# Second attention of a small decoder: two heads of each group of four are scaled by VectorE in place of GpSimd

## The chip, the cores and the metric

The kernel runs on one core of a Trainium2 chip, in one launch. The metric is the device time of that core in microseconds (us). A core has engines that work side by side, each through its own list of instructions in order, and semaphores join them: TensorE (PE in the profile, PEld its weight loads), VectorE (DVE), ScalarE (ACT), GpSimd (POOL) and SyncE (SP), which issues the DMAs.

## The reference

A decoder with two layers works on x of 8 batches x 100 tokens x 256 and a context of 8 x 361 x 256. In order: a state-space layer, a first cross attention, a mixture of 8 experts, four Mamba layers, a second cross attention, and a fake-quantised feed-forward layer, each with a residual and a layer norm behind it. The change is in the second cross attention, with 16 heads of width 16:

```
def _L1_xattn_ref(q, k, v, mask, Wq, bq, Wk, bk, Wv, bv, Wo, bo):
    ...
    scores = jnp.einsum('bhqd,bhkd->bhqk', qh, kh) / math.sqrt(D_K)
    scores = jnp.where(mask == 0, -jnp.inf, scores)
    attn = jax.nn.softmax(scores, axis=-1)
    attn = jnp.nan_to_num(attn, nan=0.0)
    x = jnp.einsum('bhqk,bhkd->bhqd', attn, vh)
    x = x.transpose(0, 2, 1, 3).reshape(bs, sq, HIDDEN)
    return x @ Wo + bo
```

## The kernel before, in words

The stages follow each other: the first attention with the experts until some 370 us into the span, the Mamba layers until some 1055, the second attention until some 1285, the feed-forward layer until the end.

Both attentions are software pipelines over heads. Four heads are a **quad**; a batch has four quads, and the 8 batches have quads 0 to 31. A quad's scores are four PSUM tiles of 100 x 361, one for each head. One step `g` of the loops `pe_attn`, `act_attn`, `dve_attn` and `pool_attn` is one head (`n, i = divmod(g, 4)`: quad n, head i), and each engine's instructions are issued in the order of these steps. In the second attention (`a.layer == 1`) the work of quad n runs as follows.

- **TensorE**, step i = 0: scores of quad n (L634, eight 32x361 products and then the mask, four bf16 products); it first waits until all four exponentials of quad n-1 are done (`a.exp_ready`), as they read the same PSUM tiles. Then the values of quad n-2 (24 products of 128x32 by 128x100). Steps 1 to 3: the transposes of quad n-1's probabilities, four a step (L705, called r0, r1, r2 here). r0 reads heads 0 and 1; r1 heads 1 and 2; r2 heads 2 and 3. They wait for the scaled heads on `a.prob_ready`, one semaphore for heads 0 and 1 and one for heads 2 and 3.
- **VectorE**, step 0: the negative maximum over heads 0 and 1 of quad n (L1088), then the scale factors for heads 2 and 3 of quad n-1 (reciprocal of the sum, L1079, and its product with a flag that is zero for a fully masked row, L1082), then the maximum over heads 2 and 3 of quad n (L1088 again). Step 2: the factors for heads 0 and 1 of quad n.
- **ScalarE**: the exponential of each head (L869, with its sum; it waits for the maximum of its pair), and between them the copies of the transposed probabilities out of PSUM (L879), in the order exp 0, exp 1, copy 0, exp 2, copy 1, exp 3, copy 2.
- **GpSimd**: multiplies each head's 100 x 361 exponentials by its factor in place (`pool_scale`, L972), heads 2 and 3 of quad n-1 in step 0 of quad n and heads 0 and 1 of quad n in step 2, each time behind `a.rs_ready`.

Beside this each batch has work at fixed steps, in every engine's own order: keys (steps 0 and 1), the mask (2), the query rows with their norm (2 to 9: L1163, the root on GpSimd L608 to L614, the end of the norm L621, a residual on GpSimd L977), values (steps 10, 13, 14; L1054 takes them out of PSUM), the output product and its norm (L1151 in step 6, L621 in step 8), the queries' copy to SBUF (L1061, step 9), the turn of a tile by TensorE (L747, steps 7 and 11), and, in steps 3 and 11 from batch 1 on until nine pieces are done, the quantising of a feed-forward weight (L2176 to L2185), all on VectorE where nothing else is said. Keys, values, queries, transposes and turned tiles share three PSUM banks in rotation; each waits until the third one before it has been read.

In the first attention VectorE scales all heads itself: reciprocal (L1073), and two `tensor_scalar` (L1076), with the same place in the order of steps. `step(ins)` lets VectorE wait until that instruction of its own has completed.

Of the kernel before, what the change touches and what calls it, by code (L numbers as in the profile page):

```python
# [5 lines left out]
ALU = mybir.AluOpType  # L6
# [8 lines left out]
B, S, D = 8, 100, 256  # L15
SK = 361
# [32 lines left out]
QUAD = 4  # L49
# [179 lines left out]
def decoder(nc, inp, out):  # L229
    ctx = ExitStack()  # L230
    with ctx:
# [3 lines left out]
        def sb(name, shape, dt=F32):  # L235
            return ctx.enter_context(nc.sbuf_tensor(name, shape, dt))
# [127 lines left out]
        anyv = sb("anyv", [P, 4])  # L364
# [11 lines left out]
        def pre(g, at):  # L376

            k, r = divmod(g - at, H)
            return (k + 1,) if r == 0 and 0 <= k + 1 < B else ()

        def fin(g, at):

            k, r = divmod(g - at, H)
            return (k - 1,) if r == 0 and 0 <= k - 1 < B else ()
# [23 lines left out]
        def has_quad(n):  # L408
            return 0 <= n < B * QUADS
# [159 lines left out]
        def step(ins):  # L569

            vstep.mark(ins)
            vstep.settle()
# [23 lines left out]
        def norm_root(pool, par, many=1, table=stat):  # L596

            G_ = nc.gpsimd
            st = table[0:S, par:par + many]
            var, v, y, t = (st[:, :, k:k + 1] for k in (7, 8, 9, 10))  # L600
            n = norms.rooted = norms.rooted + 1

            def mark(ins, k):
                ins.then_inc(n_step, 1)
                pool.wait_ge(n_step, 5 * (n - 1) + k)

            pool.wait_ge(n_stat, n)
            mark(G_.tensor_scalar(v, var, LN_EPS, 1.0, ALU.add, ALU.mult), 1)  # L608
            mark(G_.tensor_tensor(y, v, cst[0:S, 3:4].rearrange("p (o a) -> p o a", o=1).to_broadcast([S, many, 1]),
                                  ALU.pow), 2)  # L610
            mark(G_.tensor_tensor(t, y, y, ALU.mult), 3)
            mark(G_.tensor_tensor(t, t, v, ALU.mult), 4)
            mark(G_.tensor_scalar(t, t, -0.5, 1.5, ALU.mult, ALU.add), 5)
            G_.tensor_tensor(y, y, t, ALU.mult).then_inc(n_root, 1)  # L614
# [349 lines left out]

        def pool_scale(pool, a, n, i, k):

            pool.wait_ge(a.rs_ready, 2 * n + i // 2 + 1)
            for j in range(i, i + k):
                e = a.es[0:S, (n * QUAD + j) % 8, 0:SK]
                rs = hstat[0:S, n % 2, 2, j:j + 1]  # L970
                ready = a.prob_ready[j // 2]
                nc.gpsimd.tensor_scalar(e, e, rs, 1.0, ALU.mult, ALU.mult).then_inc(ready, 1)  # L972

        def gp_residual(pool, a, b):

            pool.wait_ge(a.in_ready, b + 1)
            nc.gpsimd.tensor_tensor(x_tok[:, b, :], a.x1[0:S, b % 2], bob[:, :], ALU.add).then_inc(xo2, 1)  # L977

        def pool_attn(pool, a):

            for g in a.steps:
                n, i = divmod(g, QUAD)
                if a.layer == 1 and i == 0 and has_quad(n - 1):
                    pool_scale(pool, a, n - 1, 2, 2)
                if a.layer == 1 and i == 2 and has_quad(n):
                    pool_scale(pool, a, n, 0, 2)
                if a.layer == 0:
                    for b in pre(g, AT["xo"]):
                        pool.wait_ge(xt_full, b + 1)
                        nc.gpsimd.tensor_tensor(x_tok[:, b, :], x_tok[:, b, :], bob[:, :], ALU.add).then_inc(xo_ready, 1)  # L990
                    for at in ("N1", "N2"):
                        for b in fin(g, AT[at]):
                            norm_root(pool, b % 2)
                    if g == AHEAD["gN"]:
                        gm_root_first(pool)
                        gm_rates(pool, 0)
                    if g == AHEAD["gD"]:
                        for c in range(CD):
                            gm_delta(pool, 0, 0, c)
                    if g == AHEAD["gB"]:  # L1000
                        pool.wait_ge(a.so_free, 4 * B)
                        gm_bx(pool, 0)
                else:
                    for b in pre(g, AT["1x"]):
                        norm_root(pool, b % 2)
                    for b in pre(g, AT["1xe"]):
                        gp_residual(pool, a, b)
                    for b in fin(g, AT["1N"]):
                        norm_root(pool, b % 2)
# [21 lines left out]
        def pool_front(pool):  # L1031
            pool_bias_parts(pool)
            for b in range(B):
                norm_root(pool, b % 2)
            pool.wait_ge(ld_attn, 16 * N_ATTN)
            pool_attn(pool, attn[0])
            mam_pool(pool)
            attn1_pool(pool)
            ffn_pool(pool)
# [27 lines left out]
        def dve_scale(dve, a, n, i, k):  # L1067

            dve.wait_ge(a.exp_ready, n * QUAD + i + k)
            st = hstat[0:S, n % 2]  # L1070
            if a.layer == 0:

                step(nc.vector.reciprocal(st[:, 2, i:i + k], st[:, 1, i:i + k]))  # L1073
                for j in range(i, i + k):
                    e = a.es[0:S, (n * QUAD + j) % 8, 0:SK]
                    nc.vector.tensor_scalar(e, e, st[:, 2, j:j + 1], CLIP_EPS, ALU.mult,  # L1076
                                            ALU.max).then_inc(a.prob_ready[j // 2], 1)
            else:
                step(nc.vector.reciprocal(st[:, 3, i:i + k], st[:, 1, i:i + k]))  # L1079

                bp = n // QUADS % 2
                nc.vector.tensor_scalar(st[:, 2, i:i + k], st[:, 3, i:i + k], anyv[0:S, bp:bp + 1], None,  # L1082
                                        ALU.mult).then_inc(a.rs_ready, 1)

        def dve_max(dve, a, n, i):

# [728 lines left out]
        def gm_root_first(pool):  # L1815

            s = msq[0:S]
            t, r0, tmp = s[:, 12:16], s[:, 8:12], s[:, 16:20]
            power = cst[0:S, 3:4].to_broadcast([S, GB])
            pool.wait_ge(m_rs, 1)  # L1820
            nc.gpsimd.tensor_scalar(t, s[:, 0:4], 1.0 / D, LN_EPS, ALU.mult, ALU.add).then_inc(m_root, 1)
            pool.wait_ge(m_root, 1)
            nc.gpsimd.tensor_tensor(r0, t, power, ALU.pow).then_inc(m_root, 1)
            pool.wait_ge(m_root, 2)
            nc.gpsimd.tensor_tensor(tmp, r0, r0, ALU.mult).then_inc(m_root, 1)
            pool.wait_ge(m_root, 3)
            nc.gpsimd.tensor_tensor(tmp, t, tmp, ALU.mult).then_inc(m_root, 1)
            pool.wait_ge(m_root, 4)
            nc.gpsimd.tensor_scalar(tmp, tmp, -0.5, 1.5, ALU.mult, ALU.add).then_inc(m_root, 1)
            pool.wait_ge(m_root, 5)  # L1830
            nc.gpsimd.tensor_tensor(nrm4[0:S, :], r0, tmp, ALU.mult).then_inc(m_rstd, 5)

        def gm_rates(pool, l):

            pool.wait_ge(m_alog, l + 1)
            nc.gpsimd.tensor_scalar(aneg[:, l % 2], aneg[:, l % 2], -1.0, -SLOWEST, ALU.mult, ALU.min).then_inc(m_aneg, 1)

        def gm_delta(pool, m, g, c):

            if m == 0:  # L1840
                pool.wait_ge(m_soft, 1)
            else:
                p_read(pool, m, f"D{c}")
                pool.wait_ge(m_bx, UNITS * (m - 1) + NQ * (c + 1))
            nc.gpsimd.tensor_tensor(dx[:, c], delta[g][:, c], xc[g][:, c], ALU.mult).then_inc(m_dx, 1)
            pool.wait_ge(m_dx, CD * m + c + 1)
            nc.gpsimd.memset(delta[g][:, c].rearrange("p (b t) -> p b t", b=GB)[:, :, 0:1], RESET).then_inc(m_first, 1)

        def gm_bx(pool, unit):

            m, u = divmod(unit, UNITS)
            c, nq = divmod(u, NQ)
            if c == 0:
                pool.wait_ge(m_bin[nq], 16 * (m + 1))
            wait(pool, m_scan, 2 * (unit - BX + 1))
            nc.gpsimd.tensor_tensor(  # L1856
                bx[:, unit % BX].rearrange("p (j t) -> p j t", j=SEGMENT),
                bbc[:, nq].rearrange("p (j t) -> p j t", j=SEGMENT),
                dx[:, c].rearrange("p (o t) -> p o t", o=1).to_broadcast([P, SEGMENT, GT]),
                ALU.mult).then_inc(m_bx, 1)  # L1860
# [616 lines left out]
```

## Time and profile before

| | us |
|---|---|
| median of 3 runs | 1352.81 |
| lowest, highest | 1341.77, 1353.56 |
| the profiled execution's own time | 1346.96 |
| its span, first to last instruction | 1345.1 |
| mean granted TensorE clock in it | 0.942 |
| busy: TensorE / VectorE / ScalarE / GpSimd | 1155.2 / 1092.8 / 826.3 / 820.9 |

The span is cut by the stages above; the busy times are sums over stages whose limits differ. A releaser in square brackets behind a row is what ended the idle time before it.

### The profile page before, as it was taken

The page shows a single profiled execution, that of the slowest core. Times are in us where ns is not written, and L with a number is a line of the kernel's source. Part 1 is how long each engine was busy: PE and PEld are TensorE (multiplying, and loading weights), DVE is VectorE, ACT ScalarE, POOL GpSimd, SP SyncE. Part 2 cuts the span into 40 slices and gives each one's busy share as a digit, 9 for nine tenths or more (in the row PEclk, how much of TensorE's full clock was granted, in tenths as well). Part 3 has the DMA queues.
Part 4 walks back from the last instruction along what each step waited for, and adds up shares of the span by engine and source line. Part 5 has one row for each costly group of instructions (what it writes and reads, how often), then busy time and mean ns, then how long its engine had stood idle before and what let it go on. Part 6 is the DMA issues. An engine that isn't in the chain of part 4 may idle for free.

```text
span 1345.1 us, 17666 instructions
## 1 busy us (share of the span) xinstructions
PE 1155.2 (86%) x6026; PEld 671.9 (50%) x6026; DVE 1092.8 (81%) x1618; ACT 826.3 (61%) x1825; POOL 820.9 (61%) x743
## 2 busy tenths in 40 slices
PE   7798888878579998989989989899987888888874
PEld 3455555544144554545545445455454555555544
DVE  3577777575599999999999999999999667676556
ACT  1555555564366777767777678776764355566664
POOL 6001111100498998999989989899899344445405
PEclk9899999989779999999999999999998989899885
DMA  6000002000500504106032060230500300000000
GB/s 202 12 12 12 12 12 70 1 1 3 219 15 15 225 1 169 45 0 239 1 121 92 1 240 1 80 133 1 197 31 0 80 16 17 22 27 2 1 1 25
DMA packets 22142, 79.15 MB, mean 59 GB/s; under 512 B 4935, under 2 KB 8847, under 8 KB 21138
## 3 DMA queue, kind: packets, MB, share of 16 engines
q1 hardware_dynamic: 22054, 78.02, 16.8%
q8 instruction: 49, 0.80, 0.2%
q14 instruction: 39, 0.32, 0.1%
HBM read 76.77 MB, written 1.24 MB: 58 GB/s over the span
## 4 chain that ended last, share of the span: by engine, by line
PE 38%; DVE 33%; ACT 13%; POOL 8%; issue 7%; DMA 1%; SPq 0%; ACTq 0%; DVEq 0%; POOLq 0%
PE ps L634 35%; DVE ps L1941 10%; DVE arena L1946 6%; POOL arena L1856 4%; DVE arena L1944 4%; DVE hstat L1088 3%; ACT ps L1740 3%; ACT L629 2%; ACT arena L869 2%; PE ps L705 2%; POOL arena L1868 2%; DVE arena L1906 2%; ACT arena L879 1%; DMA arena<-in_exb 1%; ACT arena L1626 1%
## 5 line engine op out<-in xcount | busy, mean ns | idle before, releaser
L634 PE MATMUL ps<-arena 128*32 128x100 f32 (+8 forms) x3300 | 522.3, 385 | 84.0 <-ACT arena L869 25.5
L1856 POOL TENSOR_TENSOR arena<-arena 128x1600 f32<-128x1600 f32 x128 | 456.5, 3581 | 34.9 <-DVE ps L1941 21.8
L634 PEld LDWEIGHTS ps<-arena 128*32 128x32 f32 (+7 forms) x3300 | 262.7, 147 | 301.8 <-issue 112.5
L634 PE MATMUL ps<-arena,ident 128*128 128x400 f32 x1024 | 378.4, 519 | 33.4 <-DVE arena L1944 17.5
L1740 ACT ACTIVATE ps<-arena 128x400 f32<-128x400 f32 x512 | 283.1, 590 | 194.4 <-DVE arena L1944 161.1
L1941 DVE TENSOR_TENSOR_SCAN ps<-ps,arena 128x800 f32<-128x800 f32 x176 | 320.7, 1822 | 18.6 <-ACT ps L1740 14.4
L634 PEld LDWEIGHTS ps<-arena,ident 128*128 128x128 f32 x1024 | 197.5, 196 | 197.3 <-POOL arena L1868 24.0
L869 ACT ACTIVATE arena<-ps,hstat 100x361 f32<-100x361 f32 x256 | 143.5, 563 | 108.5 <-DVE hstat L1088 108.3
L608 POOL TENSOR_SCALAR stat<-stat 100x1 f32<-100x1 f32 (+1 forms) x44 | 8.6, 196 | 293.3 <-DVE stat L589 292.1
L1944 DVE TENSOR_TENSOR arena<-ps,arena 128x800 f32<-128x800 f32 x176 | 174.4, 991 | 6.0
L1088 DVE TENSOR_REDUCE hstat<-ps 100x2 f32<-100x722 f32 x128 | 115.6, 905 | 75.0 <-PE ps L634 74.6
L1868 POOL TENSOR_TENSOR arena<-arena 128x1600 f32<-128x1600 f32 x40 | 143.1, 3577 | 15.1 <-DVE arena L1946 15.0
L972 POOL TENSOR_SCALAR arena<-arena,hstat 100x361 f32<-100x361 f32 x128 | 71.7, 573 | 113.3 <-DVE hstat L1082 112.3
L1946 DVE TENSOR_TENSOR_SCAN arena<-ps,arena 128x800 f32<-128x800 f32 x80 | 140.3, 1804 | 0.2 <-issue 0.2
L705 PE MATMUL ps<-ident,arena 100*128 100x100 f32 x768 | 105.6, 264 | 16.3 <-POOL arena L972 8.0
L879 ACT ACTIVATE arena<-ps 128x400 f32<-128x400 f32 x192 | 97.1, 506 | 33.8 <-PE ps L705 32.3
L705 PEld LDWEIGHTS ps<-ident,arena 100*128 100x128 f32 x768 | 82.5, 147 | 48.2 <-issue 18.4
L629 ACT ACT_TABLE_LOAD x63 | 80.8, 1283 | 1.1
L634 PE MATMUL ps<-wv,arena 128*128 128x256 f32 (+1 forms) x192 | 53.2, 402 | 5.9 <-DVE arena L1054 3.4
L869 ACT ACTIVATION_READ_ACCUMULATOR arena<-ps,hstat 100x1 f32 x256 | 52.3, 204 | 0.0
L634 PE MATMUL ps<-arena,wk 128*128 128x361 f32 x128 | 48.7, 508 | 0.7
L1076 DVE TENSOR_SCALAR arena<-arena,hstat 100x361 f32<-100x361 f32 x128 | 46.5, 406 | 2.3
(191 smaller groups left out, 1004.1 us busy)
## 6 DMA issues: line engine op xcount, KB each, us to landing
arena<-bc_scratch SPq DMA_DIRECT2D x64, 800.0 KB, 6.5
arena<-in_ctxT SPq DMA_DIRECT2D x16, 361.0 KB, 3.8
arena<-in_w_in SPq DMA_DIRECT2D x4, 1024.0 KB, 4.9
arena<-in_expT SPq DMA_DIRECT2D x1, 2048.0 KB, 12.7
arena<-in_w_out SPq DMA_DIRECT2D x4, 512.0 KB, 3.2
arena<-in_mask SPq DMA_DIRECT2D x8, 141.0 KB
arena<-in_xT SPq DMA_DIRECT2D x2, 400.0 KB, 4.1
x_tok<-in_x_tok SPq DMA_DIRECT2D x1, 800.0 KB
```

Of the source, the lines that this page charges most:

```text
L629: act.add_instruction(mybir.InstLoadActFuncSet(name=nc.get_next_instruction_name(), act_func_set_id=which, engine=mybir.EngineType.Activat ...
L634: return nc.tensor.matmul(outp, lhsT, rhs, start=first, stop=last)
L705: last = nc.tensor.transpose(ps[:, a.bank(b, name), k * S:(k + 1) * S], a.es[0:S, (n * QUAD + i) % 8, kc * P:(kc + 1) * P], ident[0:S, 0:S])
L869: nc.scalar.activation(a.es[0:S, v % 8, 0:SK], ps[0:S, i, 0:SK], ACT.Exp, bias=hstat[0:S, n % 2, 0, i:i + 1], scale=1.0, accum_out=hstat[0 ...
L879: nc.scalar.activation(a.aT[:, n % 2, r * QUAD * S:(r + 1) * QUAD * S], ps[:, a.bank(b, name), 0:QUAD * S], ACT.Copy).then_inc(a.freed(b, ...
L1088: nc.vector.tensor_reduce(hstat[0:S, n % 2, 0, i:i + 2], ps[0:S, i:i + 2, 0:SK], AX.X, ALU.max, negate=True).then_inc(a.max_ready, 1)
L1740: last = nc.scalar.activation(psf[:, half_at(k) + j * GT:half_at(k) + (j + 1) * GT], delta[g][:, c], ACT.Exp, scale=aneg[:, l % 2, n:n + 1])
L1856: nc.gpsimd.tensor_tensor(bx[:, unit % BX].rearrange("p (j t) -> p j t", j=SEGMENT), bbc[:, nq].rearrange("p (j t) -> p j t", j=SEGMENT), ...
L1868: nc.gpsimd.tensor_tensor(h, h, cbc[:, nq], ALU.mult).then_inc(m_cmp, 1)
L1941: nc.vector.tensor_tensor_scan(a, a, bx[:, unit % BX, w], 0.0, ALU.mult, ALU.add).then_inc(m_scan, 1)
L1944: nc.vector.tensor_tensor(y, a, cbc[:, nq, w], ALU.mult).then_inc(m_cmd, 1)
L1946: nc.vector.tensor_tensor_scan(y, a, bx[:, unit % BX, w], 0.0, ALU.mult, ALU.add).then_inc(m_scan, 1)
```

## The change

VectorE gives the factors of heads 0 and 1 to GpSimd as before. For heads 2 and 3 of each quad it waits for its own factor and does the two multiplications itself (step 0 of the next quad), with the completion semaphore on each of them; GpSimd leaves them out. `rs_ready` is counted once a quad. Line numbers behind L1080 move by five, those inside `dve_scale` otherwise: the reciprocal is L1077 and the factor L1080 in the changed kernel, the new multiplications L1088, the maxima L1093.

```
         def pool_scale(pool, a, n, i, k):
-            pool.wait_ge(a.rs_ready, 2 * n + i // 2 + 1)
+            pool.wait_ge(a.rs_ready, n + 1)
             for j in range(i, i + k):
                 e = a.es[0:S, (n * QUAD + j) % 8, 0:SK]
                 rs = hstat[0:S, n % 2, 2, j:j + 1]
...
                 n, i = divmod(g, QUAD)
-                if a.layer == 1 and i == 0 and has_quad(n - 1):
-                    pool_scale(pool, a, n - 1, 2, 2)
                 if a.layer == 1 and i == 2 and has_quad(n):
                     pool_scale(pool, a, n, 0, 2)
...
-                nc.vector.tensor_scalar(st[:, 2, i:i + k], st[:, 3, i:i + k], anyv[0:S, bp:bp + 1], None,
-                                        ALU.mult).then_inc(a.rs_ready, 1)
+                scale = nc.vector.tensor_scalar(st[:, 2, i:i + k], st[:, 3, i:i + k], anyv[0:S, bp:bp + 1], None,
+                                                ALU.mult)
+                if i == 0:
+                    scale.then_inc(a.rs_ready, 1)
+                    return
+                step(scale)
+                for j in range(i, i + k):
+                    e = a.es[0:S, (n * QUAD + j) % 8, 0:SK]
+                    nc.vector.tensor_scalar(e, e, st[:, 2, j:j + 1], None, ALU.mult).then_inc(a.prob_ready[j // 2], 1)
```

On VectorE, around step 0 of the second quad of a batch (L621 there ends the norm of the query rows; `hstat` holds the maxima and factors, `arena` the exponentials). Before:

```order
L2185 TENSOR_SCALAR arena<-arena 88x1024
L1088 TENSOR_REDUCE hstat<-ps 100x2
L1079 RECIPROCAL hstat<-hstat 100x2
L1082 TENSOR_SCALAR hstat<-hstat,anyv 100x2
L1088 TENSOR_REDUCE hstat<-ps 100x2
L621 TENSOR_SCALAR arena<-arena,stat 100x256
L1079 RECIPROCAL hstat<-hstat 100x2
L1082 TENSOR_SCALAR hstat<-hstat,anyv 100x2
L1151 TENSOR_TENSOR arena<-ps,x_tok 100x256
```

And in the changed kernel:

```order
L2190 TENSOR_SCALAR arena<-arena 88x1024
L1093 TENSOR_REDUCE hstat<-ps 100x2
L1077 RECIPROCAL hstat<-hstat 100x2
L1080 TENSOR_SCALAR hstat<-hstat,anyv 100x2
L1088 TENSOR_SCALAR arena<-arena,hstat 100x361 x2
L1093 TENSOR_REDUCE hstat<-ps 100x2
L621 TENSOR_SCALAR arena<-arena,stat 100x256
L1077 RECIPROCAL hstat<-hstat 100x2
L1080 TENSOR_SCALAR hstat<-hstat,anyv 100x2
L1156 TENSOR_TENSOR arena<-ps,x_tok 100x256
```

The two multiplications stand between the two maxima of every quad but the first (and behind the last quad's factors at the end); nothing else on VectorE moves.

On GpSimd, the same place, from the end of the root of the query rows' norm. Before:

```order
L614 TENSOR_TENSOR stat<-stat 100x1
L972 TENSOR_SCALAR arena<-arena,hstat 100x361 x2
L977 TENSOR_TENSOR x_tok<-arena,bob 100x256
L972 TENSOR_SCALAR arena<-arena,hstat 100x361 x2
L608 TENSOR_SCALAR stat<-stat 100x1
```

And in the changed kernel:

```order
L614 TENSOR_TENSOR stat<-stat 100x1
L977 TENSOR_TENSOR x_tok<-arena,bob 100x256
L972 TENSOR_SCALAR arena<-arena,hstat 100x361 x2
L608 TENSOR_SCALAR stat<-stat 100x1
```

The first pair of L972 has gone there; the pair for heads 0 and 1 stays where it was.

## Rows read from the trace of the kernel before

**Rows 1.** The page: the chain that ended last, share of the span by engine.
```profile
PE 38%; DVE 33%; ACT 13%; POOL 8%; issue 7%; DMA 1%; SPq 0%; ACTq 0%; DVEq 0%; POOLq 0%
```

**Rows 2.** Windows, the second attention: length, busy (instructions) by engine, clock, DMA.
```profile
1060.00:1283.00 223.00, 189.90 (x1797) 126.14 (x1796) 148.93 (x381) 128.44 (x391) 100.79 (x219) 0.93 0.09 25
```

**Rows 3.** Waits, 1060 to 1290: waiter <- releaser: total us, times, longest.
```profile
PE ps L634 <- ACT arena L869: 11.4, 9, 1.4
PE ps L705 <- POOL arena L972: 8.0, 10, 1.1
PE ps L747 <- DVE arena L1151: 4.6, 6, 0.8
```

**Rows 4.** Timeline, quad 30: start, us, engine, line, operation [idle before <-releaser].
```profile
1268.61 0.91 DVE L1088 TENSOR_REDUCE hstat<-ps 100x2 f32<-100x722 f32 x1 [1.98 <-PE ps L634]
1269.43 0.15 DVE L1079 RECIPROCAL hstat<-hstat 100x2 f32<-100x2 f32 x1
1269.55 0.56 ACT L869 ACTIVATE arena<-ps,hstat 100x361 f32<-100x361 f32 x1 [2.25 <-DVE hstat L1088]
1269.62 0.23 DVE L1082 TENSOR_SCALAR hstat<-hstat,anyv 100x2 f32<-100x2 f32 x1
1269.76 0.90 DVE L1088 TENSOR_REDUCE hstat<-ps 100x2 f32<-100x722 f32 x1
1269.96 1.12 POOL L972 TENSOR_SCALAR arena<-arena,hstat 100x361 f32<-100x361 f32 x2 [1.32 <-DVE hstat L1082]
...
1270.58 1.02 PE L705 MATMUL ps<-ident,arena 100*128 100x100 f32 x6 [0.69 <-POOL arena L972]
...
1271.03 0.57 ACT L869 ACTIVATE arena<-ps,hstat 100x361 f32<-100x361 f32 x1
...
1271.94 0.59 ACT L869 ACTIVATE arena<-ps,hstat 100x361 f32<-100x361 f32 x1
...
1272.67 0.87 PE L634 MATMUL ps<-arena 32*100 32x361 f32 x8 [0.90 <-ACT arena L869]
```

**Rows 5.** Timeline, first attention, one step 0 and one L621.
```profile
72.89 0.73 DVE L1076 TENSOR_SCALAR arena<-arena,hstat 100x361 f32<-100x361 f32 x2
...
73.54 0.90 DVE L1088 TENSOR_REDUCE hstat<-ps 100x2 f32<-100x722 f32 x1
...
80.96 0.40 DVE L621 TENSOR_SCALAR arena<-arena,stat 100x256 f32<-100x256 f32 x1
```

**Rows 6.** Timeline, quad 13, second of its batch.
```profile
1157.82 0.64 DVE L621 TENSOR_SCALAR arena<-arena,stat 100x256 f32<-100x256 f32 x1
...
1159.76 0.57 PE L747 MATMUL ps<-ident,arena 100*128 100x100 f32 x2 [0.77 <-DVE arena L1151]
```

**Rows 7.** Timeline, quads 14 and 22, third of their batches.
```profile
1166.08 0.43 DVE L1061 SCALAR_TENSOR_TENSOR arena<-ps,bq,head_rows 128x200 f32<-128x200 f32 x1 [0.26 <-PE ps L634]
...
1166.68 0.43 DVE L1061 SCALAR_TENSOR_TENSOR arena<-ps,bq,head_rows 128x200 f32<-128x200 f32 x1 [0.17 <-PE ps L634]
...
1220.12 0.74 DVE L1061 SCALAR_TENSOR_TENSOR arena<-ps,bq,head_rows 128x200 f32<-128x200 f32 x2
...
1220.58 1.13 PE L634 MATMUL ps<-wv,arena 128*128 128x256 f32 x4
```

**Rows 8.** Timeline, end of quad 23, fourth of its batch, and quad 24.
```profile
1227.14 0.59 ACT L869 ACTIVATE arena<-ps,hstat 100x361 f32<-100x361 f32 x1
...
1227.96 0.87 PE L634 MATMUL ps<-arena 32*100 32x361 f32 x8
```

**Rows 9.** Timeline, quad 12, first of its batch, and the scores of quad 13.
```profile
1150.47 0.17 DVE L1079 RECIPROCAL hstat<-hstat 100x2 f32<-100x2 f32 x1 [1.15 <-ACT arena L869]
...
1151.38 0.55 ACT L869 ACTIVATE arena<-ps,hstat 100x361 f32<-100x361 f32 x1
...
1153.01 0.87 PE L634 MATMUL ps<-arena 32*100 32x361 f32 x8 [1.44 <-ACT arena L869]
```

**Rows 10.** One line's instructions (min/median/max ns): L1076 in the first attention.
```profile
L1076 DVE TENSOR_SCALAR arena<-arena,hstat x128: 396/406/441, 43.3 to 330.9; 100x361 f32<-100x361 f32 x128
```

## The prediction

> **What bounds the kernel now.** I read the page's chain first: the work that ended last is shared by TensorE with 38% and VectorE with 33% [rows 1]. Such shares mix stages, so I cut out the stage of the change with the windows view. In its 223 us TensorE is busy 189.9 us (85%), VectorE 148.9, GpSimd 100.8 [rows 2]. TensorE has 33 us without a matmul, and the view of waits tells for whom: 11.4 us for the exponentials L869, 8.0 us for GpSimd's scaling L972, 4.6 us for L1151 on VectorE before a turn [rows 3]. The 8.0 us are what the change is aimed at. Whether they are worth anything is read from the timeline of a quad.
>
> Quad 30 is a clean one [rows 4]. I count from the start of its first maximum at 1268.61. Factors for heads 2 and 3 of the quad before start at +1.01, the second maximum at +1.15, the third exponential at +2.42, the fourth at +3.33; it ends at +3.92, and the scores of the next quad start at +4.06, 0.14 behind it. TensorE waited 0.69 for GpSimd in this quad, and still stood 0.90 before the next scores, waiting for an exponential. So here the chain maximum, four exponentials, scores sets the pace, and the wait for GpSimd lies inside it. The change puts work between the two maxima of that chain.
>
> **The price of the two multiplications on VectorE.** The factor L1082 starts at +1.01 and takes 0.23, and a dependent VectorE instruction starts 0.04 behind the end of the one that it waits for (1269.43 + 0.15 to 1269.62) [rows 4]: the multiplications start at +1.28. The first attention has the same multiplication on the same shape, with one more operation: 406 ns each [rows 10], and from the start of two of them to the next maximum 0.65 (72.89 to 73.54) [rows 5]. The second maximum then starts at +1.93 where it started at +1.15: **0.78 us later** in every quad. From a maximum's start to its exponential is 0.94 (1268.61 to 1269.55) [rows 4]; the third exponential can start at +2.87 in place of +2.42: **0.45 later**, as the remaining 0.33 was slack on ScalarE. What is bought: head 2 is ready at about +1.28 + 0.41 = +1.69, where GpSimd's first half of 1.12 us from +1.35 ended at +1.91; r1 can start 0.2 earlier.
>
> A rule that would make it cheaper is in the Trainium skill, GPSIMD Engine Reference, Key points: VectorE is about twice as fast for elementwise work. By it two heads would take half of GpSimd's 1.12, 0.56 in place of the 0.65 that the row shows, and each quad's delay would shrink by 0.09, the sum by some 2 us. The first attention's rows, 406 against some 560 ns a head, speak against two to one, and I go by them.
>
> **A gain on the side.** L621, a multiplication with two scalars, takes 0.64 while GpSimd's L972 runs beside it, as in quad 13 [rows 6], and 0.40 in the first attention, where GpSimd stands idle at that moment [rows 5]. L621 follows the second maximum in the second and third quad of each batch. With the pair for heads 2 and 3 gone from GpSimd it should take 0.40: 0.24 back. GpSimd's own queue gets shorter by 64 instructions of some 560 ns; but it waits for VectorE nearly everywhere, so that is worth nothing by itself. DMAs and SyncE are not touched.
>
> **Quad by quad.** The pattern repeats with the batch; I went through all 32 quads in the timeline.
>
> - *First quad of a batch* (4, 8, ..., 24: six). Keys keep TensorE and ScalarE busy: the third exponential starts at 1151.38, 4.11 behind the first maximum, and VectorE stands idle 1.15 before its next factor [rows 9]. Both covers are wider than 0.78. Cost 0. Were the cover gone, it would be 0.45 each.
> - *Second quad* (5, 9, ..., 25: six). VectorE goes without a gap from the second maximum through L621, the factors and L1151, and the turn on TensorE waits 0.77 for it at 1159.76 [rows 6]; six times in the stage [rows 3]. The next scores come straight behind. So the 0.78 lands whole, less the 0.24 of L621: 0.54. The exponentials' way gives less. 6 x 0.54 = 3.24.
> - *Third quad* (10, 18, 22, 26). L621 is followed by L1061, whose first half ends at about 1220.53, and the product for the values, which needs that bank, starts at 1220.58 [rows 7]. Again 0.54: 4 x 0.54 = 2.16. In quads 6 and 14 TensorE was at half clock and VectorE waited twice for it there, 0.26 and 0.17 in quad 14 [rows 7], so about 0.54 - 0.26 - 0.17, or 0.12, is left: 0.24. Quad 2 has no L621, and L1061 had more room: 0.23. Together 2.63.
> - *Fourth quad* (3, 7, ..., 27: seven). The last exponential ends at 1227.73, the scores start at 1227.96 [rows 8], 0.23 behind in place of the least 0.14: slack 0.09. 0.45 - 0.09 = 0.36; 7 x 0.36 = 2.52.
> - *The last batch* (28, 30, 31) has the clean chain of quad 30: 3 x 0.45 = 1.35. In 29 ScalarE is late by itself: 0. In quads 0 and 1 the stage is still filling: 0.
>
> Sum: 3.24 + 2.63 + 2.52 + 1.35 = **9.7 us slower**. The profiled execution took 1346.96, 1.9 more than its span, which the change leaves alone: 1356.7. The median shown, 1352.81, lies 5.9 above the profiled one, for a reason that this page doesn't show; from it the sum gives 1362.5. I take the middle, **1360**. Against either base it is +0.7%. A difference of about 1% (13.5 us) is what a measurement of this kernel tells from none.
>
> The granted clock is 0.93 here [rows 2]; halved pieces of it fall on some quads. A slower chain may move them, by a few us either way. I put no sum on it, only range.
>
> **The rivals.**
>
> *A. GpSimd's lateness set the pace: faster.* TensorE did wait 8.0 us in ten places for L972 [rows 3]. If those waits, and not the exponentials, decided, and VectorE had room, the change would take away up to those 8.0 us, and 14 times 0.24 of L621, 3.4: -11.4, 1335.6 on the profiled base, 1341 on the median. It decides if the second maximum is not what the third exponential waits for, so if ScalarE is the later one by over 0.78. Against it: in quad 30 the maximum ended at 1270.66 and the exponential started at 1271.03, only 0.37 behind, and the wait before the scores came after the one for GpSimd [rows 4]. Half of this effect beside some of the cost would give about no change. Chance 0.15.
>
> *B. Everything lands.* VectorE has stretches without a gap before the maxima (L2185 and then L1088 in the order shown). If the slacks are used up once the whole pattern shifts, each quad pays 0.78: 32 x 0.78 = +25, 1372 on the profiled base, 1378 on the median. Against it: the idle 1.15 and the late exponentials in the first quads [rows 9], which recur in each batch whatever the rest does. Chance 0.15.
>
> *C. The multiplications are slower here than in the first attention*, where GpSimd rests. As L621 stretched from 0.40 to 0.64, each could take 0.24 more, the delay 1.26 in place of 0.78, and the sum some 9.7 x 1.26 / 0.78 = 15.7 and a little more: 1363 to 1369. It needs a GpSimd instruction beside them; but at +1.28 to +2.0 only the pair that is removed ran there [rows 4], and roots and residuals lie elsewhere. Chance 0.06.
>
> The Trainium skill, GPSIMD Engine Reference, Key points, has the contention with VectorE in its two-port mode, which is what the 0.64 of L621 would be; it says nothing of how much.
>
> *D. The change does nothing visible*, since TensorE, busy 85%, catches up in the first quad of each batch, whose TensorE stands idle 1.44 before the scores [rows 9]. But that idle time waits for an exponential that itself waits for TensorE's work, so it moves with the start of the quad. Sum 0: 1347 to 1353. Chance 0.07.
>
> My forecast, +6 to +13, has the remaining 0.57.
>
> **Range and chances.** Runs of the kernel before lie between 1341.77 and 1353.56, so the forecast's own range is 1351 to 1367. With D and the upper half of A taken in below and most of B above: 1347 to 1374. Slower by over 1%: B 0.15, most of C 0.05, and 0.08 of the forecast by spread, together 0.28. Faster by over 1%: only A in full, 0.04. Within 1%: 0.68.
>
> **What the profile after should show.** L1088 (the new one) 64 times at about 406 ns, starting 0.27 behind the start of L1080. From the first maximum of a quad to the second 1.93 in place of 1.15. Third exponential at +2.87 in the clean quads; in the first quads of batches still near +4.1. L621 at 0.40 instead of 0.64 in the stage. The waits of L705 for L972 nearly gone, those of L634 for L869 longer, the turn L747 behind L1156 waiting 0.5 longer. The stage about 10 us longer, nothing changed before 1060 and behind it. Wrong would be: exponentials that start as before (A), gaps of VectorE gone in the first quads (B), multiplications near 640 ns (C), or a stage as long as before (D).

## The result, and the profile after

The changed kernel took 1358.79 us in the median of 13 runs beside 1346.93 for the kernel before: ratio 1.0096, 95% interval 1.0074 to 1.0117. That is some 13 us slower, between 10 and 16. A second comparison gave 1.0096 again (1.0072 to 1.0121). The ratios are of fast runs; one run of the kernel before took 1524.38 us and is left out of them. The prediction said +9.7 us on either base, 1360 with 1347 to 1374, and 0.68 for "within 1%". The direction was right and the sum too small. Two things came out better than the sum by luck. The 1360 stood on a base of some 1350, the middle between 1346.96 and the 1352.81 of the first three runs, which is 3 us above the 1346.93 of thirteen; that made up for the 3 us missing from the sum. And 0.96% lies just inside "within 1%", with an interval that reaches beyond it.

The profiled span went from 1345.1 to 1357.3 us. Quad 30 after, in the timeline, answers to [rows 4] (L1156 of the changed kernel is the L1151 of before, L1059 the L1061, L1052 the L1054):

```profile
1277.66 0.91 DVE L1093 TENSOR_REDUCE hstat<-ps 100x2 f32<-100x722 f32 x1 [1.99 <-PE ps L634]
...
1278.67 0.23 DVE L1080 TENSOR_SCALAR hstat<-hstat,anyv 100x2 f32<-100x2 f32 x1
1278.94 0.72 DVE L1088 TENSOR_SCALAR arena<-arena,hstat 100x361 f32<-100x361 f32 x2
...
1279.40 0.79 PE L705 MATMUL ps<-ident,arena 100*128 100x100 f32 x6 [0.47 <-DVE arena L1088]
1279.58 0.90 DVE L1093 TENSOR_REDUCE hstat<-ps 100x2 f32<-100x722 f32 x1
...
1280.40 0.40 DVE L621 TENSOR_SCALAR arena<-arena,stat 100x256 f32<-100x256 f32 x1
1280.52 0.56 ACT L869 ACTIVATE arena<-ps,hstat 100x361 f32<-100x361 f32 x1 [0.32 <-DVE hstat L1093]
...
1282.16 0.56 PE L634 MATMUL ps<-arena 32*100 32x361 f32 x4 [0.91 <-ACT arena L869]
```

Counted from the first maximum at 1277.66, the multiplications start at +1.28, the second maximum at +1.92, and the third exponential at +2.86; ScalarE is now idle before it, waiting for that maximum. The next scores start at +4.50 where they started at +4.06. The transposes of head 2, the second part of r1, start at +1.74 in place of +1.97, and that buys nothing: TensorE stands as long before the scores as it did (0.91). L621 takes 0.40 where it took 0.64. The waits of the stage answer to [rows 3]:

```profile
PE ps L634 <- ACT arena L869: 16.2, 16, 2.0
PE ps L747 <- DVE arena L1156: 7.8, 6, 1.3
PE ps L705 <- DVE arena L1088: 5.5, 9, 0.8
```

TensorE's wait for the scaled heads fell from 8.0 us (for GpSimd) to 5.5 (for VectorE); its waits for exponentials rose by 4.8 and the turn's by 3.2. The three places of the prediction, in the timeline of the changed kernel, a second and a third quad [rows 6, 7]:

```profile
1249.90 0.36 PE L747 MATMUL ps<-ident,arena 100*128 100x100 f32 x2 [1.29 <-DVE arena L1156]
...
1254.90 0.75 DVE L1059 SCALAR_TENSOR_TENSOR arena<-ps,bq,head_rows 128x200 f32<-128x200 f32 x2
...
1255.37 1.13 PE L634 MATMUL ps<-wv,arena 128*128 128x256 f32 x4 [0.38 <-DVE arena L1059]
```

The turn waits 1.29 where it waited 0.77, and the value product now waits for L1059. The end of a fourth quad and a first quad [rows 8, 9]:

```profile
1235.61 0.56 ACT L869 ACTIVATE arena<-ps,hstat 100x361 f32<-100x361 f32 x1
...
1236.41 0.87 PE L634 MATMUL ps<-arena 32*100 32x361 f32 x8 [0.55 <-ACT arena L869]
...
1241.26 0.17 DVE L1077 RECIPROCAL hstat<-hstat 100x2 f32<-100x2 f32 x1 [0.38 <-ACT arena L869]
...
1243.81 0.56 PE L634 MATMUL ps<-arena 32*100 32x361 f32 x4 [1.44 <-ACT arena L869]
```

In the first quad VectorE is still idle for 0.38 us of the 1.15, and TensorE's wait is the 1.44 of before: the cover held.

**A table of periods.** A period is the time from the first maximum of a quad to that of the next, in us, from the timelines, in quads of which no part ran at half clock. The quad's number is in brackets. Batch 6 (quads 24 to 27) is free of the quantising that lengthens other quads; "clean" is quad 30, or quads 28 and 29 where 30 was partly at half clock.

| kernel | first (24) | second (25) | third (26) | fourth (27) | clean |
|---|---|---|---|---|---|
| before | 7.40 | 5.86 | 6.22 | 5.80 | 5.71 |
| the change | 7.40 | 6.39 | 6.76 | 6.24 | 6.15 |
| heads 2, 3 unscaled | 7.39 | 5.71 | 6.13 | 5.80 | 5.72 |
| both maxima first | 7.39 | - | - | 5.83 | 5.74 |
| L1151 moved (GpSimd scales) | 7.40 | 5.71 | 6.22 | 5.80 | 5.71 |
| all three ways | 7.40 | 5.74 | 6.44 | 5.83 | 5.74 |
| multiplied twice | 7.40 | - | - | 6.87 | - |

"-" marks quads that were partly at half clock there.

### The profile page after: what moved, and what is told of

Read it like the earlier page. It is cut to its first block, busy times and chain, and to the rows that moved or that the text cites. A ratio compares the mean times of both kernels' runs of the same rounds, so it can differ in the third digit from the quotient of the medians.

```text
span 1357.3 us, 17666 instructions
## 1 busy us (share of the span) xinstructions
PE 1157.3 (85%) x6026; PEld 673.2 (50%) x6026; DVE 1111.7 (82%) x1682; ACT 828.1 (61%) x1825; POOL 786.2 (58%) x679
## 4 chain that ended last, share of the span: by engine, by line
PE 38%; DVE 37%; ACT 13%; issue 7%; POOL 4%; DMA 1%; SPq 0%; ACTq 0%; DVEq 0%; POOLq 0%
PE ps L634 35%; DVE ps L1946 10%; DVE arena L1951 7%; DVE hstat L1093 5%; DVE arena L1949 4%; ACT ps L1745 3%; ACT L629 2%; POOL arena L1861 2%; ACT arena L869 2%; PE ps L705 2%; DVE arena L1911 2%; DVE arena L1088 1%; ACT arena L1631 1%; POOL arena L1873 1%; ACT arena L879 1%
## 5 line engine op out<-in xcount | busy, mean ns | idle before, releaser
L634 PE MATMUL ps<-arena 128*32 128x100 f32 (+8 forms) x3300 | 522.2, 384 | 87.7 <-ACT arena L869 30.7
L1861 POOL TENSOR_TENSOR arena<-arena 128x1600 f32<-128x1600 f32 x128 | 456.5, 3581 | 34.7 <-DVE ps L1946 21.5
L634 PEld LDWEIGHTS ps<-arena 128*32 128x32 f32 (+7 forms) x3300 | 263.2, 147 | 304.9 <-issue 110.8
L634 PE MATMUL ps<-arena,ident 128*128 128x400 f32 x1024 | 378.3, 519 | 33.6 <-DVE arena L1949 17.5
L634 PEld LDWEIGHTS ps<-arena,ident 128*128 128x128 f32 x1024 | 197.5, 196 | 197.4 <-POOL arena L1873 24.1
L869 ACT ACTIVATE arena<-ps,hstat 100x361 f32<-100x361 f32 x256 | 143.2, 562 | 116.6 <-DVE hstat L1093 116.5
L1093 DVE TENSOR_REDUCE hstat<-ps 100x2 f32<-100x722 f32 x128 | 115.6, 904 | 75.8 <-PE ps L634 75.4
L705 PE MATMUL ps<-ident,arena 100*128 100x100 f32 x768 | 104.1, 263 | 15.4 <-DVE arena L1088 5.5
L972 POOL TENSOR_SCALAR arena<-arena,hstat 100x361 f32<-100x361 f32 x64 | 36.3, 580 | 138.2 <-DVE hstat L1080 137.3
L705 PEld LDWEIGHTS ps<-ident,arena 100*128 100x128 f32 x768 | 81.7, 146 | 46.7 <-issue 18.2
L634 PE MATMUL ps<-wv,arena 128*128 128x256 f32 (+1 forms) x192 | 54.2, 408 | 9.0 <-DVE arena L1052 3.5
L869 ACT ACTIVATION_READ_ACCUMULATOR arena<-ps,hstat 100x1 f32 x256 | 51.5, 201 | 0.0
L634 PE MATMUL ps<-arena,wk 128*128 128x361 f32 x128 | 49.9, 518 | 0.7
```

Source lines behind the costliest of these rows:

```text
L634: return nc.tensor.matmul(outp, lhsT, rhs, start=first, stop=last)
L705: last = nc.tensor.transpose(ps[:, a.bank(b, name), k * S:(k + 1) * S], a.es[0:S, (n * QUAD + i) % 8, kc * P:(kc + 1) * P], ident[0:S, 0:S])
L869: nc.scalar.activation(a.es[0:S, v % 8, 0:SK], ps[0:S, i, 0:SK], ACT.Exp, bias=hstat[0:S, n % 2, 0, i:i + 1], scale=1.0, accum_out=hstat[0 ...
L1093: nc.vector.tensor_reduce(hstat[0:S, n % 2, 0, i:i + 2], ps[0:S, i:i + 2, 0:SK], AX.X, ALU.max, negate=True).then_inc(a.max_ready, 1)
L1861: nc.gpsimd.tensor_tensor(bx[:, unit % BX].rearrange("p (j t) -> p j t", j=SEGMENT), bbc[:, nq].rearrange("p (j t) -> p j t", j=SEGMENT), ...
```

## The experiments

All ratios are to the kernel before, run beside them, with 95% intervals. The code shows the part of each edit that matters; "..." marks lines left out.

**Both maxima first.** In `dve_quad`, second attention only:

```
+            if i == 0 and has_quad(n) and a.layer == 1:
+                dve_max(dve, a, n, 2)
             if i == 0 and has_quad(n - 1):
                 dve_scale(dve, a, n - 1, 2, 2)
...
```

> The changed kernel with one thing moved: in the second attention both maxima of a quad stand ahead of the factors and multiplications for heads 2 and 3 of the quad before. My account has two ways in which the multiplications cost: through the second maximum to the third exponential (fourth quads of a batch 0.36 each, last batch 0.45 each, some 3.9 us together), and through VectorE's own queue to L1156 and L1059, for which TensorE waits (second and third quads, some 5.8 us). The first way should be gone: third exponential back at +2.42 from the first maximum, fourth quads back to 5.8 us, the kernel some 4 us faster than the changed one and still some 6 us slower than before. r1 waits longer, as head 2 is ready only at about +2.5, which may give back up to 0.2 us a quad in the last batch. Rival, that added VectorE time costs by its amount wherever it stands: as slow as the changed kernel, +12. Rival, that only the exponentials' way counts: equal to before.

Measured: 1.0075 (1.0045 to 1.0105), +6 to +14 us. In its timeline a fourth quad:

```profile
1254.98 1.73 DVE L1093 TENSOR_REDUCE hstat<-ps 100x2 f32<-100x722 f32 x2 [1.63 <-PE ps L634]
...
1257.08 0.73 DVE L1088 TENSOR_SCALAR arena<-arena,hstat 100x361 f32<-100x361 f32 x2
1257.39 0.57 ACT L869 ACTIVATE arena<-ps,hstat 100x361 f32<-100x361 f32 x1
```

The third exponential is back at +2.41 though VectorE does the same work, and the fourth and clean quads are back at 5.83 and 5.74. So the first way, through the second maximum, is shown by the periods. By time alone it is not: the run lies between the expected +6 and the change's +13, and its interval reaches both. In its profile all six second quads ran partly at half clock.

**Heads 2 and 3 left unscaled**, the factor signals TensorE:

```
-                step(scale)
-                for j in range(i, i + k):
-                    ...
+                scale.then_inc(a.prob_ready[1], 2)
```

> Heads 2 and 3 of each quad are scaled by no engine (this part of the computation is left out); the factor itself signals TensorE. It tells what GpSimd's scaling of these heads cost in the kernel before, and so the most that any mover of it could win. My account: TensorE's 8.0 us of waits for GpSimd lie inside the exponentials' chain and are worth nothing; what comes back is L621 at 0.40 in place of 0.64, in six second quads and four third ones, so 2.4 us faster than before, third exponential at +2.42 as before. Rival A of the prediction (GpSimd's lateness set the pace): 8 to 11 us faster than before.

Measured: 0.9981 (0.9960 to 1.0002), -2.6 us where -2.4 was expected. The agreement is closer than the mechanism allows: L621 is back at 0.40, but the second quads have 5.71 in place of 5.86, 0.15 less and not 0.24, and the third quads are 0.09 to 0.16 shorter (6.13 in place of 6.22 in quad 26, 7.25 in place of 7.41 in quad 14, against the kernel before once more). By periods that is some 1.7 us. The rest is as before. In its waits L705 no longer waits for GpSimd, and L634's wait for exponentials is 12.4 us where it was 11.4 [rows 3]:

```profile
PE ps L634 <- ACT arena L869: 12.4, 9, 2.0
...
PE ps L705 <- ACT arena L879: 7.3, 12, 0.8
```

Rival A, 8 to 11 us faster, falls: the interval ends at 5.4 us faster. By the periods, the scaling of these heads had some 1.7 us to give, wherever it is moved, and not the 8.0 of the view of waits.

**The multiplications done twice**, first into scratch:

```
...
+                    vstep.mark(nc.vector.tensor_scalar(hh[0:S, IC - 4 + j, 0:SK], e, st[:, 2, j:j + 1], None, ALU.mult))
...
```

> The changed kernel with the two multiplications of VectorE done twice, first into a scratch tile. Second maximum at +2.66 in place of +1.92 (0.73 more). My account: second quads 6 x 0.73, third quads 6 x 0.73, fourth quads 7 x 0.73, last batch 3 x 0.73, together 16.1; in the first quads VectorE's idle time of 0.38 is used up and 0.35 is over, which counts in the five batches in which VectorE goes on without a gap to the next quad's maximum: 1.8. So 18 us slower than the changed kernel, the third exponential at +3.6 in clean quads and still near +4.1 in first quads. Rival B (everything lands): 32 x 0.73 = 23. Rival, that most of the change's cost has nothing to do with the multiplications' time (an offset of another origin): clearly less than 18.

Measured: 1.0289 (1.0249 to 1.0329), 26 us above the change. The second pair costs 0.63 a quad in the order of VectorE, not 0.73 (starts at 1282.36 and 1282.99), and the fourth quads went from 6.24 to 6.87, so one for one:

```profile
1282.36 0.73 DVE L1088 TENSOR_SCALAR arena<-arena,hstat 100x361 f32<-100x361 f32 x2
...
1282.99 0.72 DVE L1091 TENSOR_SCALAR arena<-arena,hstat 100x361 f32<-100x361 f32 x2
...
1283.63 0.90 DVE L1096 TENSOR_REDUCE hstat<-ps 100x2 f32<-100x722 f32 x1
...
1284.57 0.56 ACT L869 ACTIVATE arena<-ps,hstat 100x361 f32<-100x361 f32 x1 [0.96 <-DVE hstat L1096]
```

For five of the first quads my expectation was 0.35; those with quantising that ran at full clock became 0.15 to 0.17 longer (quad 4: 9.00 in place of 8.84), and quad 24 kept its 7.40. By full-clock periods that makes some 15 us. In the profile the stage is 25 us longer than in the change's first profile and 21.5 longer than in its second; what goes beyond 15 lies in quads at half clock, of which there were 52 us here, against 17 and 37.5. My expectation of 18 had no term for that. By time alone the 26 is nearer to rival B's 23 than to my 18; the periods of the first quads speak against B.

**One instruction moved in the kernel before**: L1151 ahead of the factors for heads 0 and 1.

```
             for g in steps:
+                if a.layer == 1:
+                    for b in fin(g, AT["1N"]):
+                        dve_resid_add(dve, a, b)
                 dve_quad(dve, a, g)
```

> The kernel before (GpSimd scales all heads), with one instruction moved: in step 6 of a batch the addition that takes the output product out of PSUM (L1151) stands ahead of the factors for heads 0 and 1, not behind them. In the kernel before the turn on TensorE waits for it 0.77 in six second quads. It could start at the end of L621, 1158.46 in place of 1159.20 in quad 13, so 0.74 earlier: 6 x 0.74 = 4.4 us faster than before, if nothing else holds the turn; the turn also needs L621's result, which is there by then. Rival: the six waits are covered by something else (exponentials, which leave 0.35 in the second quads), then 6 x 0.35 = 2.1 at most. Rival, no effect, since the factors and GpSimd's scaling of heads 0 and 1 come 0.4 later and hold r0: 0 or slower.

Measured: 0.9986 (0.9960 to 1.0012). The turn no longer waits, but the scores behind it now wait 0.61 for an exponential, and the second quads end at 5.71:

```profile
1235.15 0.41 DVE L1151 TENSOR_TENSOR arena<-ps,x_tok 100x256 f32<-100x256 f32 x1
...
1235.70 0.36 PE L747 MATMUL ps<-ident,arena 100*128 100x100 f32 x2
...
1236.68 0.87 PE L634 MATMUL ps<-arena 32*100 32x361 f32 x8 [0.61 <-ACT arena L869]
```

My account, 4.4 us, was wrong. The first rival of the expectation holds, with 0.15 a quad in place of 0.35: a wait of 0.77 was worth 0.15, since the next one stood close behind. No quad of the kernel before gets below 5.71, the clean chain.

**The change once more.**

> The changed kernel as it is, once more. Two questions. The size: my sum is 9.7 us; the first comparison gave a ratio of 1.0096, 12.9 us. And where the profiled execution's 12.2 us lay: 2.2 before the second attention begins, 7.3 within it and 2.7 behind its last maximum. My account: only the part within belongs to the change, and it would be 9.3 with the clock's halved pieces of before; the parts before and behind are spread between executions, behind it with the length of half clock (0.2 us for each us of it). So here the quads at full clock should have the same periods to 0.02 us (7.40, 6.39, 6.76, 6.24 from first to fourth), and the parts before and behind should differ from 2.2 and 2.7. Rival, that the change costs something outside its stage: again some +2 and +3.

Measured: 1.0096 (1.0072 to 1.0121); full-clock periods the same to 0.01. The attention began at 1064.75 (before 1060.21, the first profile of the change 1062.40, all others 1058.1 to 1063.2, among them four with VectorE's multiplications at 1058.7 to 1060.0): spread, as far as this shows. But the part behind the last quad's first maximum was 73.5 us again, where I had expected it to differ: for that part the rival is not refuted. In the two profiles of the kernel before it was 70.8 and 71.8. See the point on the clock in the next section.

**GpSimd busy beside VectorE's multiplications**, on scratch:

```
...
+                if a.layer == 1 and i == 0 and has_quad(n - 1):
+                    pool.wait_ge(a.rs_ready, 2 * (n - 1) + 2)
+                    ...
+                        nc.gpsimd.tensor_scalar(hh[0:S, IC - 2 + j, 0:SK], hh[0:S, IC - 3, 0:SK], cst[0:S, 3:4], 1.0,
+                                                ALU.mult, ALU.mult).then_inc(beside, 1)
...
```

> The changed kernel, and GpSimd again does two multiplications of 100 x 361 at the old moment (behind the factor for heads 2 and 3), on scratch that nobody reads. So GpSimd works beside VectorE's two multiplications, which the prediction's rival C priced at 0.24 more for each. My account: L1088's successor shows some 640 ns in place of 406 (as L621 beside GpSimd did), the second maximum at some +2.4 in place of +1.92, and the kernel slower than the changed one by 0.48 in second, third and fourth quads and the last batch: 22 x 0.48 = 11 us. GpSimd's pair is over before L621, which stays near 0.40. Rival, that only some of VectorE's instructions are stretched beside GpSimd and this one not: same as the changed kernel.

Measured: 1.0136 (1.0113 to 1.0158), 5 us above the change, where I had expected 11. In the timeline (L1096 is the L1088 of the changed kernel, L988 GpSimd's new pair):

```profile
1265.09 1.04 DVE L1096 TENSOR_SCALAR arena<-arena,hstat 100x361 f32<-100x361 f32 x2
1265.14 1.41 POOL L988 TENSOR_SCALAR arena<-arena,cst 100x361 f32<-100x361 f32 x2 [2.22 <-DVE hstat L1087]
...
1266.97 0.56 ACT L870 ACTIVATE arena<-ps,hstat 100x361 f32<-100x361 f32 x1 [0.63 <-DVE hstat L1101]
```

The two multiplications take 1.04 together in place of 0.73, and GpSimd's two 1.41 in place of 1.12: both are stretched. Not each of them, though: VectorE's first, which starts 0.06 ahead of GpSimd's, takes 0.41 as it does alone, and its second 0.72. That is why the stretch is 0.31 a quad and not the 0.48 that I took from L621; the fourth quads went from 6.24 to 6.55. L621 stayed at 0.40. The mechanism of rival C exists, and the change doesn't meet it, since GpSimd's pair is gone. The Trainium skill, GPSIMD Engine Reference, Key points, says that GpSimd shares its SBUF interfaces with VectorE and contends with VectorE's instructions in a two-port mode. The run agrees that such instructions contend; which mode VectorE was in, no view shows.

**VectorE scales only where its work falls in a first quad** (`n % QUADS == QUADS - 1`), GpSimd all the rest. GpSimd's side of it:

```
...
-                if a.layer == 1 and i == 0 and has_quad(n - 1):
+                if a.layer == 1 and i == 0 and has_quad(n - 1) and n % QUADS:
...
```

> The kernel before, with VectorE scaling heads 2 and 3 only where its work falls in the first quad of a batch (the heads of the fourth quad before it, and at the very end), all other heads on GpSimd. It tests the cover of the first quads, in which the prediction set the cost at 0. My account: within 1 us of before, first quads 7.40 at full clock as before, though their second maximum starts 0.78 later; third exponential still at +4.1. Rival, that the delay is handed on through VectorE's gapless stretch to the next maximum: first quads 0.4 to 0.8 longer, 3 to 5 us.

Measured: 0.9991 (0.9969 to 1.0013). First quads 8.84, 8.60, 8.59, 8.14, 7.72, 7.40, each within 0.01 of before. So the cost of 0 there is shown. In the timeline the idle 0.38 is what is left of the cover:

```profile
1226.58 0.73 DVE L1096 TENSOR_SCALAR arena<-arena,hstat 100x361 f32<-100x361 f32 x2
1227.22 0.90 DVE L1101 TENSOR_REDUCE hstat<-ps 100x2 f32<-100x722 f32 x1
...
1228.50 0.17 DVE L1086 RECIPROCAL hstat<-hstat 100x2 f32<-100x2 f32 x1 [0.38 <-ACT arena L876]
```

**All three ways**, with VectorE doing all that it does in the change: both maxima first, L1151's addition early, and in the third quads

```
...
                     for b in pre(g, AT["1Qc"]):
                         dve_q(dve, a, b, b % 2)
+                    for b in fin(g - 1, AT["1Ne"]):
+                        norm_end(dve, b % 2, a.zt[0:S, b % 2], a.x2[0:S, b % 2], a.x_ready)
...
```

> VectorE does all that it does in the changed kernel, in an order that keeps it off the three paths I named: both maxima ahead of the multiplications, L1151's addition ahead of the factors for heads 0 and 1, and in the third quads the queries' copy (L1061 before) ahead of L621. My account: second quads 5.74 at full clock (before 5.86, change 6.39), third 6.4 (before 6.22, change 6.76), fourth 5.83 (before 5.80, change 6.24): in all within 1 us of before, some 9 to 12 faster than the change. Rival, that VectorE's added 24 us of work cost by their amount wherever they stand: as slow as the change.

Measured: 1.0016 (0.9992 to 1.0039). In batch 6 the periods are as expected, 5.74, 6.44, 5.83. The same 64 multiplications on the same engine cost 2 us here (-1 to 5) and 13 in the change. This is the strongest of the runs: most of the cost is the place in the order, not the added work itself. The first two ways are closed by it. The third is only shortened: in quad 26 L1059 starts at +2.74 (1244.32), where the change has +3.06, and the period is 0.22 above that of before. And a third quad with quantising gains nothing from the order. Of these, quad 14 ran at full clock here:

```profile
1161.43 1.73 DVE L1093 TENSOR_REDUCE hstat<-ps 100x2 f32<-100x722 f32 x2 [1.22 <-PE ps L634]
...
1168.90 0.69 DVE L2203 TENSOR_SCALAR arena<-arena 88x1024 bf16<-88x1024 f32 x1
1169.51 1.71 DVE L1093 TENSOR_REDUCE hstat<-ps 100x2 f32<-100x722 f32 x2
```

It has 8.08, where the kernel before has 7.41 and the change, by quad 6 with the same work, 7.96. In all three kernels VectorE has no gap in such a quad from one maximum to the next. There the added work costs 0.55 in one order and 0.67 in the other.

No version is faster than the kernel before by what could be measured: this one is not, and L1151 alone moved (0.9986) and VectorE in first quads only (0.9991) have 1 inside their intervals.

**Maxima first in the last batch alone.**

> The changed kernel, with both maxima ahead of the multiplications in the last batch alone (quads 28 to 31). In both profiles of the change, the part from the last quad's first maximum to the last norm's end of the attention took 16.0 us in place of 14.1, with 10.2 us of half clock in place of 3.4, and the feed-forward layer 57.5 in place of 56.6; my sum had 0.45 there. With both maxima first everywhere that part took 12.7, with no half clock. My account: quads 28, 30 and 31 get their 0.45 back (1.3 us), the last part goes back to 12.7 to 14.1 and the feed-forward layer to 56.6: together 3 to 5 us faster than the change, ratio to before about 1.006 to 1.007. Rival, that the drain's 2.3 us of half clock come from all the 24 us that VectorE's work was made longer, or from chance: only 1.3 us faster than the change, the last part still at 16.

Measured: 1.0116 (1.0075 to 1.0157), not faster than the change. In its profile the last part was 14.85 in place of 16.0 and the feed-forward layer 56.9 in place of 57.5: shorter, but not the 12.7 to 14.1 and 56.6 that I expected, and the time of the kernel doesn't bear even that out. Inconclusive.

**The kernel before once more.**

> The kernel before, once more, as the measure of what two profiles of the same program differ by. Expected: ratio 1.000 within 0.003, full-clock periods 7.40, 5.86, 6.22, 5.80 to 0.02, the part behind the last first maximum near 70.7, and the start of the attention somewhere between 1058 and 1062.

Measured: 0.9984 (0.9960 to 1.0008). Its periods agree, but its attention took 209.7 us where the first profile has 214.1:

```profile
1061.80:1271.50 209.70, 178.28 (x1724) 117.66 (x1726) 145.43 (x373) 123.49 (x377) 97.55 (x213) 0.97 0.10 26
```

The mean clock was 0.97 and 0.94 in that stretch (half clock for 11.6 and 27.3 us). The same program differs by 4 us in this stage, and all but some hundredths of it lies in quads that ran partly at half clock in one of the two or in both. The attention began at 1061.84, and the part behind the last quad's first maximum took 71.8 us where I had expected 70.7.

## Why the prediction was right, and what was mis-sized

- *What the change is aimed at.* Right: most of the 8.0 us of waits for GpSimd lay inside the exponentials' chain. The unscaled run gives 1.7 us by periods and 2.6 (-0.3 to 5.4) by time for them and L621's part together.
- *The price a quad.* Second maximum at +1.93, measured +1.92; third exponential at +2.87, measured +2.86; multiplications of 406 ns, measured 406 (400 to 411). L621 at 0.40, measured 0.40.
- *First quads: 0.* Right, in the change and where VectorE scales only there.
- *Second quads: 0.54.* Measured 0.53 (5.86 to 6.39). With L621's 0.24 taken off whole this is right, though the unscaled run, in which L621 is shorter too, won only 0.15: there the exponentials' way came next.
- *Third quads: 0.54, with 0.12 for quads 6 and 14.* 0.54 measured in 26, and 0.31 in quad 2 (5.96 to 6.27), for which I had 0.23. The 0.12 was wrong: VectorE's waits in quads 6 and 14 came from TensorE's half clock in that one execution. At full clock quad 14 of the kernel before has 7.41 (kernel before once more) and quad 6 of the change, with the same work, 7.96: 0.55 each, 0.86 more in all. What holds in these two is also another thing than the value product: VectorE works without a gap, and its next maximum starts 1.2 us after the scores that it reads are there. A stretch at half clock is no place to read slack from.
- *Fourth quads: 0.36.* Measured 0.44. I took 0.23 minus the least 0.14 between last exponential and scores as slack. The scores of the change wait for that exponential, [0.55 <-ACT arena L869], and still start 0.24 behind its end (1235.61 + 0.56 to 1236.41). The distance is 0.23 in all seven fourth quads of the kernel before, the change, and "both maxima first" alike, and 0.14 in the last batch; why it is longer is not known. So it was no slack: 7 x 0.08 = 0.56 more.
- *Last batch: quads 28, 30, 31, and 0 for 29.* At half clock in the profile, quad 29 looked late by itself; at full clock it has 5.72 before (kernel before once more). By the clean 6.15 of quad 30 it costs 0.43: 0.43 more.
- *The sum.* With these, at full clock: 6 x 0.53 + 6 x 0.54 + 0.31 (quad 2) + 7 x 0.44 + 4 x 0.43 = 11.5 us, against 9.7 predicted and 10 to 16 measured. The profiles bear out the part up to the last quad, 11.1 of it: from the first maximum of quad 0 to that of quad 31 it was 214.1 and 209.7 us before, 221.4 and 225.2 in the change, 11.4 more in the mean.
- *The clock, given range and no sum.* The remaining 1 to 2 us fit it, but are not settled. The window from the last first maximum to the end of the attention, before and in the two profiles of the change, in that order:

```profile
1274.30:1288.40 14.10, 9.96 (x148) 7.86 (x148) 3.84 (x12) 8.10 (x20) 4.83 (x12) 0.88 0.00 1
```
```profile
1283.80:1299.80 16.00, 11.64 (x148) 9.34 (x148) 5.21 (x16) 8.00 (x20) 2.63 (x8) 0.68 0.01 2
```
```profile
1290.00:1305.90 15.90, 11.66 (x148) 9.36 (x142) 5.17 (x16) 7.95 (x19) 2.61 (x8) 0.68 0.01 2
```

  It is 1.8 to 1.9 us longer, with 0.43 of it accounted for and the clock at 0.68 in place of 0.88. But the kernel before once more had 0.62 there and took 14.8, and the run made to test it did not get faster. Whether the change draws half clock onto this part, or two profiles fell alike, stays open.
- *Rivals.* A fell to the unscaled run. B fell to the first quads' unchanged periods, though quad 14 shows that a quad without a gap in VectorE's order pays in either order. C's mechanism is real but not met. D fell to 1.0096, with an interval that begins at 1.0074.

## What to carry to other kernels

The same work on the same engine cost 13 us or 2, by its place: before moving work to an engine with idle time, look at what stands behind it in that engine's order, and put it behind whatever another engine is waiting for. Where the engine has no gap at all, as in quad 14, neither order tried was free. A view of waits gives a wait's length, not its worth; the worth is what is gained before the next wait sets in (0.77 was worth 0.15 here). Read slack only in stretches at full clock. Take a gap between two steps as slack only if it gets smaller when the step before it is late: the 0.23 here did not.

## What the runs showed of the hardware

VectorE and GpSimd stretch each other on SBUF to SBUF multiplications with two such instructions each: 0.73 to 1.04 us for VectorE's pair, 1.12 to 1.41 for GpSimd's, with VectorE's first, which started ahead, not stretched (0.41) and its second at 0.72; L621 went from 0.64 to 0.40 when GpSimd's pair left. VectorE's maximum over PSUM was not stretched beside GpSimd's pair: 0.90 (1269.76) as in the changed kernel without it (1279.58). TensorE ran at 1.2 GHz for between 10 and 52 us of this one stage in twelve profiles, and two profiles of the same program differed by 16 us of it and 4 us of time (the kernel before), and by 20 and 4 (the change). The doubled multiplications had the most of it, and TensorE was idle longest there (51 us of the stage, 30 to 45 in the others); this is one profile, and no run tests whether the one brings the other.
